# Layer 1 attention and its experts moved from two blocks of the program into one unrolled block

## What is computed

```python
xn = layernorm(x)
# attention: 16 heads of 16 features
xa = ln1(xn)
q, k, v = heads(xa @ wq), heads(xa @ wk), heads(xa @ wv)
probs = softmax(q @ k.T / sqrt(256))
s = merge(probs @ v) + xa
# experts: 2 of 8 for each token, and one shared expert
w_full = softmax over the top 2 of xn @ Wr * SCALE
h = (xn @ W1[e]) * silu(xn @ W3[e])
f = sum_e (h @ W2[e]) * w_full[e] + shared(xn)
x = x + s * silu(f)
```

## Time and profile before

| what | value |
|---|---|
| times of three runs, us | 2135.24, 2135.78, 2128.12 (median 2135.24) |
| the profiled execution, us | 2123.32, span 2121.7 |
| mean granted clock of TensorE | 0.905 of full |
| busy share of the span | PE 80%, DVE 55%, ACT 40%, POOL 25% |
| attention: first maxima to last matmul of a group | 1091.9 to 1602 us |
| experts: first transposes to the last indirect write | 1609.0 to 2063.1 us |
| finish | 2070.6 to 2121.7 us |

### The profile page before, as it was taken

The page is one execution under the profiler, slowest core; times in us unless marked ns, Lnnn a source line. Parts: engine busy times, 40 slices in busy tenths (PEclk is TensorE's granted clock), DMA queues, the critical chain, the costliest instruction groups (busy, mean ns, idle before and its releaser), DMA issues. The chain is left out here.

```text
span 2121.7 us, 24658 instructions
## 1 busy us (share of the span) xinstructions
PE 1699.5 (80%) x8146; PEld 1105.1 (52%) x8146; DVE 1175.5 (55%) x2114; ACT 850.9 (40%) x1509; POOL 529.8 (25%) x579
## 2 busy tenths in 40 slices
PE   4458999999998499999628888888776999999960
PEld 2336666666666355655302223222224888888850
DVE  3435545654565234343367677777753655666635
ACT  1124444444444121222105556666663544445421
POOL 1122524253434212212024420000000333333330
PEclk8679999999999799999858889999987999999985
DMA  4433444544433444343254542332313555555537
GB/s 132 139 110 99 100 117 114 147 105 117 96 110 60 130 152 152 140 168 119 80 129 120 147 127 78 82 86 75 89 29 100 143 148 140 144 135 128 148 60 237
DMA packets 223458, 251.08 MB, mean 118 GB/s; under 512 B 35984, under 2 KB 172688, under 8 KB 223376
## 3 DMA queue, kind: packets, MB, share of 16 engines
q1 hardware_dynamic: 193616, 208.54, 32.4%
q0 software_dynamic: 29760, 41.50, 11.1%
HBM read 153.34 MB, written 96.10 MB: 118 GB/s over the span
## 5 line engine op out<-in xcount | busy, mean ns | idle before, releaser
L1244 DVE TENSOR_REDUCE a_neg_max<-a_bank 128x1 f32<-128x512 f32 x512 | 328.4, 684 | 93.8 <-PE a_bank L1147 85.7
L1224 ACT ACTIVATE a_prob<-a_bank 128x512 f32<-128x512 f32 x512 | 278.6, 598 | 244.2 <-PE a_bank L1158 226.4
L1158 PE MATMUL a_bank<-a_qa,a_ka 50*128 50x512 f32 x512 | 135.5, 525 | 90.8 <-ACT a_prob L1224 61.0
L1476 POOL DMA_INDIRECT fs<-e_y,e_token x92 | 143.3, 1557 | 243.7 <-issue 232.5
L1147 PE MATMUL a_bank<-a_ka,a_qa 48*128 48x512 f32 x512 | 127.3, 491 | 39.6 <-DMA a_va<-v 29.3
L1577 DVE TENSOR_TENSOR e_h<-e_bank,e_sg 128x512 f32<-128x512 f32 x92 | 63.6, 692 | 167.3 <-ACT e_sg L1542 164.4
L1167 PE MATMUL a_bank<-a_prob,a_va 128*32 128x512 f32 x1024 | 155.2, 734 | 1.2 <-ACT a_prob L1224 1.2
L1158 PEld LDWEIGHTS a_bank<-a_qa,a_ka 50*128 50x128 f32 x512 | 50.7, 193 | 200.7 <-ACT a_prob L1224 111.0
L1542 ACT ACTIVATE e_sg<-e_bank 128x512 f32<-128x512 f32 x92 | 55.0, 597 | 222.3 <-PE e_bank L92 222.3
L648 POOL DMA_INDIRECT f<-e_ye,c_slot_row x64 | 101.0, 1579 | 72.7 <-issue 47.6
L895 PE MATMUL p_bank<-p_xnT,p_ws 128*128 128x512 f32 x256 | 111.2, 592 | 0.0
(11 more groups left out here) (311 smaller groups left out, 4075.4 us busy)
## 6 DMA issues: line engine op xcount, KB each, us to landing
e_raw<-in_W SPq DMA_DIRECT2D x69, 512.0 KB
e_raw<-in_w SPq DMA_DIRECT2D x48, 512.0 KB, 5.6
a_qa<-qk SPq DMA_DIRECT2D x192, 64.0 KB
a_ka<-qk SPq DMA_DIRECT2D x192, 64.0 KB
xs<-c_pad SPq DMA_DIRECT2D x23, 516.0 KB
e_xg<-xs SPq DMA_DIRECT2D x23, 516.0 KB, 3.7
qk<-p_hi SPq DMA_DIRECT2D x32, 256.0 KB, 2.0
qk<-p_lo SPq DMA_DIRECT2D x32, 256.0 KB, 2.0
```

Source lines behind the costliest of these rows:

```text
L1158: nc.tensor.matmul(SB[(c + s) % 3][:], ka[q][rows, p, j * P:(j + 1) * P], qa[q][rows, p, :], start=True, stop=True).then_inc(s_ps, 1)
L1224: nc.scalar.activation(prob[j][:, 2 * p + s, :], SB[(c + s) % 3][:], ACT.Exp, scale=float(D) ** -0.5).then_inc(p_done, 1)
L1244: nc.vector.tensor_reduce(neg_max[:, g % 2, at_:at_ + 1], MB[(c + s) % 3][:], AX.X, ALU.max, negate=True).then_inc(mx_done, 1)
L1476: nc.gpsimd.indirect_dma_start(f_rows, bass.IndirectOffsetOnAxis(token[u][:, t:t + 1], 0), y[:, t, :], None, compute_op=ALU.add).then_inc( ...
```

## The change

Both blocks become `layer1_attend_and_experts` (line 1169 of the new kernel), with all loops written out. GpSimd first scatters the rows of all 8 sequences (into `xg`, the buffer that later holds an expert group's rows). Head group g carries expert group e = g - 8 (FIRST = 8): eight *slots*, in each a score pair, a maxima pair or the turn of the maxima, and an eighth of an expert group. The down products of an expert group run one head group late. So head groups 0 to 7 carry no expert, 8 to 30 carry e = 0 to 22, and 31 carries the last down products.

With both sets of tiles in memory at once, buffers shrink: the maxima have one pair of banks (`M`, reduced as one 128x2x512 instruction; the experts' transposes use it too), the scores one pair (`S2`, one exponential of 128x1024), prob two tiles for four, qa/ka/va three for four. Silu becomes 0.5 g (1 + tanh(g / 2)), whose Tanh is on ScalarE and whose factor 0.5 went into the routing weights (line 1137), so VectorE has one more product a chunk. The low parts of the weights move from VectorE to GpSimd (line 1314), the weighting of y from VectorE to ScalarE (line 1541). The attention's result is no longer stored and loaded: GpSimd adds it to `xa_all` (`add_o`, line 1300), from two tiles `o`. `x1`, kept in on-chip memory before, is stored by `layer1_prepare` (line 829) and loaded by `finish`.

The diff, cut to its core (helpers whose body is as before are left out):

```diff
-def layer1_attention(nc, R, k, qk_v, v_v, o_v, xn_b, xs_rows):
-def layer1_experts(nc, R, k, xs_g, f_rows, w1_d, w2_d, w3_d):
+def layer1_attend_and_experts(nc, R, k, qk_v, v_v, xn_b, xs_rows, xs_g, f_rows, w1_d, w2_d, w3_d):
...
+    G, NU, NR = NB * NQ, 2 * T, 3
+    FIRST = G - 1 - NG
+    M, S2 = [R.ctx.enter_context(nc.psum_tensor(R.tag + n, [P, 2, 512], F32)) for n in ("max_bank", "score_bank")]
+    OB, YB, GATE, VALUE = R.banks(4)
...
         @block.sync
         def _(sp):
...
+            for g in range(G):
+                e = g - FIRST
+                if g + 2 < G:
+                    load_qk(g + 2)
+                if group(e + 1):
+                    load_w(0, e + 1)
+                    load_w(1, e + 1)
+                if g + 2 < G:
+                    load_v(g + 2)
+                if g + 1 < G:
+                    max_rows(g + 1)
+                if group(e + 1):
+                    load_w(2, e + 1)
+                    if e + 1 == 0:
+                        load_x(0)
+                if group(e + 2) and e + 1 >= 0:
+                    load_x(e + 2)
...
         @block.gpsimd
         def _(pool):
+            def scatter_rows(b):
+                if b:
+                    pool.wait_ge(rows_out, b * TOP * T * 16)
+                pool.dma_start(xg[:, :, 0:D], at(xn_b, b)).then_inc(rows_in, 16)
+                nc.gpsimd.tensor_copy(xg[:].bitcast(I32)[:, :, D], k.token[:, b * T:(b + 1) * T]).then_inc(marked, 1)
+                for i in range(TOP):
+                    if i:
+                        pool.wait_ge(rows_out, (TOP * b + i) * T * 16)
...
+            for b in range(NB):
+                scatter_rows(b)
+            added = 0
+            for g in range(G + 2):
+                e = g - FIRST
+                if group(e - 2):
+                    combine(e - 2, 1)
+                if group(e):
+                    low_w(2, e)
+                if e >= -1:
+                    while added < min(g, G):
+                        add_o(added)
+                        added += 1
+                if group(e - 1):
+                    combine(e - 1, 0)
+                if group(e + 1):
+                    low_w(0, e + 1)
+                    low_w(1, e + 1)
+                    marks(e + 1)
...
         @block.tensor
         def _(pe):
...
+            def weigh(g, j):
+                if j == 0:
+                    pe.wait_ge(v_in, 16 * (g + 1))
+                    pe.wait_ge(o_done, g)
...
+                scores(g, 0)
+                maxima(g + 1, 4)
+                if group(e):
+                    up_gate(e, 0)
+                    up_value(e, 0)
+                maxima(g + 1, 5)
+
+                scores(g, 1)
+                if g:
+                    weigh(g - 1, 3)
+                if group(e - 1):
+                    down(e - 1, 0)
+                maxima(g + 1, 6)
+
+                scores(g, 2)
+                if group(e):
+                    up_gate(e, 1)
+                maxima(g + 1, 7)
+                if g:
+                    transpose_o(g - 1)
+                if group(e):
+                    up_value(e, 1)
+
+                scores(g, 3)
+                if group(e - 1):
+                    down(e - 1, 1)
+                transpose_max(g + 1)
+
+                scores(g, 4)
+                weigh(g, 0)
+                if group(e):
+                    up_gate(e, 2)
+                maxima(g + 2, 0)
+                if group(e):
+                    up_value(e, 2)
+                maxima(g + 2, 1)
...
+                scores(g, 7)
+                weigh(g, 2)
+                if group(e + 1):
+                    transpose_x(e + 1)
+                if group(e - 1):
+                    down(e - 1, 3)
...
         @block.vector
         def _(dve):
...
+            def divide(g):
+                dve.wait_ge(oT_ps, g + 1)
+                v = OB[:].rearrange("p (t h d) -> p (t h) d", t=T, h=QH)
+                nc.vector.reciprocal(den[:], v[:, :, HD]).then_inc(den_done, 1)
+                dve.wait_ge(den_done, g + 1)
+                if g >= 2:
+                    dve.wait_ge(xa_done, g - 1)
+                nc.vector.tensor_tensor(o[:, g % 2].rearrange("p t (h d) -> p (t h) d", d=HD), v[:, :, 0:HD],
+                                        den[:].unsqueeze(2).broadcast_to([P, T * QH, HD]), ALU.mult).then_inc(o_done, 1)
```

More of the change, by code:

```diff
@@ new lines, in add_o, with marks @@
+            def add_o(g):
+                b, q = divmod(g, NQ)
+                pool.wait_ge(o_done, g + 1)
+                part = k.xa_all[:, b, :, q * QH * HD:(q + 1) * QH * HD]
+                nc.gpsimd.tensor_tensor(part, part, o[:, g % 2], ALU.add).then_inc(xa_done, 1)
+            def marks(e):
+                pool.wait_ge(xg_in, 16 * (e + 1))
+                if e >= 4:
+                    pool.wait_ge(f_out, 16 * GT * (e - 3))
+                    pool.wait_ge(y_done, 2 * (e - 3))
+                land(pool, k)
+                nc.gpsimd.tensor_copy(token[e % 4][:], xg[:].bitcast(U32)[:, :, D])
+                nc.gpsimd.tensor_copy(weight[e % 4][:], xg[:, :, D + 1]).then_inc(marks_set, 1)
@@ new lines, in transpose_max, with scores @@
+            def transpose_max(g):
+                if g >= G:
+                    return
+                pe.wait_ge(mx_done, NU * (g + 1))
+                nc.tensor.transpose(M[0:QH * T, 0, 0:P], neg_max[:, g % 2].rearrange("p s m -> p (s m)"), k.ident[:]).then_inc(mT_ps, 1)
+            def scores(g, u):
+                q, (j, p) = g % NR, divmod(u, 2)
+                if u == 0:
+                    pe.wait_ge(m_in, 4 * 16 * (g + 1))
+                if g or u:
+                    pe.wait_ge(p_done, NU * g + u)
+                for s in range(2):
+                    rows = slice(HALF * s, HALF * s + KR)
+                    nc.tensor.matmul(S2[:, s, :], ka[q][rows, p, j * P:(j + 1) * P], qa[q][rows, p, :], start=True, stop=True).then_inc(s_ps, 1)
@@ new lines, in _ @@
+            pe.wait_ge(k_set, 1)
+            for m in range(NU):
+                maxima(0, m)
+            transpose_max(0)
+            for m in range(4):
+                maxima(1, m)
+            for g in range(G):
+                e = g - FIRST
+                scores(g, 0)
[30 more added lines that the diff above has]
+                maxima(g + 2, 1)
+                scores(g, 5)
+                weigh(g, 1)
+                if group(e - 1):
+                    down(e - 1, 2)
+                maxima(g + 2, 2)
+                scores(g, 6)
+                if group(e):
+                    up_gate(e, 3)
+                maxima(g + 2, 3)
+                if group(e):
+                    up_value(e, 3)
+                scores(g, 7)
+                weigh(g, 2)
+                if group(e + 1):
+                    transpose_x(e + 1)
+                if group(e - 1):
+                    down(e - 1, 3)
@@ L1592, in _ @@
-            low_w(0, 0)
-            low_x(0)
-            turns(dve, turn)
-def finish(nc, R, k, fs_b, at_b, out_b):
+            for i in range(NR):
+                for s in range(2):
+                    ins = nc.vector.memset(ka[i][HALF * s + 32:HALF * s + 64].bitcast(F32), 1.0)
+            ins.then_inc(k_set, 1)
+            for m in range(NU):
+                maxima(0, m)
+            split_max(0)
+            for m in range(4):
+                maxima(1, m)
+            for g in range(G):
+                e = g - FIRST
+                maxima(g + 1, 4)
+                if group(e):
+                    hidden(e, 0)
+                maxima(g + 1, 5)
+                if group(e):
+                    low_h(e, 0)
+                maxima(g + 1, 6)
+                maxima(g + 1, 7)
+                if g:
+                    divide(g - 1)
+                if group(e):
+                    hidden(e, 1)
+                split_max(g + 1)
+                if group(e):
+                    low_h(e, 1)
+                maxima(g + 2, 0)
+                if group(e):
+                    hidden(e, 2)
+                maxima(g + 2, 1)
+                if group(e):
+                    low_h(e, 2)
+                maxima(g + 2, 2)
+                maxima(g + 2, 3)
+                if group(e):
+                    hidden(e, 3)
+                if group(e + 1):
+                    low_x(e + 1)
+                if group(e):
+                    low_h(e, 3)
```

677 lines of the change are left out of this document (287 added, 390 removed).

## The result

| | before | changed |
|---|---|---|
| median of 4 runs | 2131.68 us (2124.80 to 2135.78) | 2245.25 us (2241.68 to 2252.87) |
| ratio | | 1.0528, 95% interval 1.0495 to 1.0562 |
| profiled execution | 2123.32 us, span 2121.7 | 2245.51 us, span 2243.8 |
| mean granted clock of it | 0.905 | 0.867 |

The change makes the kernel 5.3% slower: 114 us. The forecast was 2080 us, 52 us faster, and its range ended at 2130.

What follows compares the result with a forecast made beforehand. TensorE was taken to bound the fused group at 27.0 us. Stall release at 1247, groups 4 to 7 and 23 fused groups, tail and finish gave span 2066, 56 us less, so about 2080 us; range 2035 to 2130.

Steps and rivals of the forecast that it cites:

- the one on the lock: Fused groups: GpSimd's low_w and VectorE's low_h miss each other by 0.3 to 2 us, so priced at nothing extra.
- my walk: Slot-by-slot walk of one fused group: 27.0 us of TensorE work plus waits of 0.5, 0.2 and 0.4, given as 27.9.
- the 0.9: Fused groups: 0.9 us a group added for waits that a slot-by-slot count misses.
- rival 1: Fused groups: two low_w hold a low_h each, 4.8 us a group, 110 us more, 2190 us; chance 0.06.
- 28.8 forecast: Time of a fused group, 28.8 us against 33.8 one after the other; 23 of them gain 115 us.
- the 158 us above: Account of the 23 fused groups: forecast 657 us, measured 815, difference +158.
- Half overlap: Fused groups: hand-overs cost more than walked, 30.5 to 31.7 us a group, 2119 to 2147 us; chance 0.10.
- 18.3 us: Head groups without an expert: assumed time per group, four of them costing 13 us more than at 15.0.
- The half-clock end: Head groups without an expert: 22.4 us each if TensorE runs at half clock, against 16.8 at full clock.
- the 26 us: Account from stall release to the first fused group, 4.5 groups: forecast 82 us, measured 108, difference +26.
- the stall: divide(2) waits for the first add_o behind GpSimd's row writes: about 1180 to 1247, some 65 us with TensorE idle.
- The bound of 31.7 us a group: Sign against the forecast: it is wrong if fused groups take over 31.7 us.

Runs made afterwards that it cites:

- the gate: Changed kernel with GpSimd's low_w(2, e) held back by a wait until low_h of the first chunk is done: 2136.28 us (before 2126.51).
- the kernel with adjacent products: Kernel with own results, low_w(2) wait and second maxima banks, plus value products right behind gate products in slots 2 and 6: 2051.86 us, ratio 0.9625.
- the second pair: Changed kernel with idle gate and value banks taking every second maxima pair in head groups 0 to 7: 2230.27 us (before 2129.33).
- all three mended: Changed kernel with idle tiles for first results, low_w(2) behind low_h, and second maxima banks in groups 0 to 7: 2047.44 us, ratio 0.9632.

## Why the prediction was wrong

**The step that failed** is the one on the lock: "In my walk they miss each other by 0.3 to 2 us, so I price it at nothing beyond the 0.9". A walk by durations with some 2 us of error a group can't say that two instructions of 0.7 and 2.4 us miss by 0.3. They met in 22 of 23 groups. The argument with which rival 1 got 0.06, that in a fixed phase held ones drift apart, is contradicted too: the delay holds TensorE and so moves the whole group, the next one included, and in 20 groups GpSimd's record starts 0.49 to 0.53 us behind VectorE's. Rival 1 is what happened, but that its price of 4.8 us a group, taken for two collisions, is so near the 4.74 measured is luck: it was one collision, 2.9 us of wait, and 2.2 for the clock behind it, together 5.15, and two of the 23 groups lost nothing (e = 1, held for 2.5 us, and e = 4). 4.74 x 23 = 109, as the gate gave back. The rows of before had shown the pair with GpSimd as the one held; that it also goes the other way round stood only on the page of the Trainium skill that the prediction cites. The traces show both ways: GpSimd's copies held, and VectorE held where GpSimd's subtraction starts first (2.47 us). But in the 20 groups VectorE's record starts 0.5 us ahead and VectorE is the one held, so "whichever starts first" does not describe the order of these records.

The walk's sum had a slip besides: 27.0 + 0.5 + 0.2 + 0.4 is 28.1, not 27.9, 0.2 us a group.

**TensorE's own work was too small.** In the kernel with the gate TensorE is 99% busy and still takes 30.8 us, against 28.8 forecast: the missing 2.0 are 46 us over the kernel. So of the 158 us above some 109 are the lock and 49 this. A pattern of its rows:

```profile
1815.79 0.50 PE L92 MATMUL a_bank<-a_xThi,a_w31hi 128*128 128x512 f32 x1
1816.12 0.39 PE L92 MATMUL a_bank<-a_xTlo,a_w31hi 128*128 128x512 f32 x1
1816.35 0.40 PE L92 MATMUL a_bank<-a_xThi,a_w31lo 128*128 128x512 f32 x1
...
1817.38 0.50 PE L1364 MATMUL a_max_bank<-a_ka,a_qa 48*128 48x512 f32 x2
```

Matmuls start 0.23 apart inside a run, as I had counted, but 0.33 after a change of the kind of work. The run of six from 1815.79 to 1817.38 takes 1.59, not 6 x 0.2255 = 1.35; runs of twelve down products take 1.54 to 1.62, not 1.42; a set of `weigh` 0.99, not 0.87. A fused group has 35 such runs, the old expert group three changes of kind, and a price of 0.1 each, an estimate from these starts, gives 3.5 of the 3.7 between 27.0 and 30.7; the wait of 0.23 in front of a maxima pair is the rest. In the kernel with adjacent products four runs took 0.1 less each, which fits; nothing else tests this price. My 0.9 for "waits that such a walk misses" was to cover this, and "Half overlap" (30.5 to 31.7 a group) was the right case for it.

**The groups without an expert were mis-sized.** I took 18.3 us between 16.8 and 22.4, "nearer to the full clock, as in the old attention (0.89)". Groups 4 to 7 took 23 to 25 at 0.55. Order of time, TensorE, in that stretch of the changed kernel:

```profile
1262.94 0.80 PE L1363 MATMUL a_max_bank<-a_ka,a_qa 48*128 48x512 f32 x2 [1.42 <-DVE a_neg_max L1601]
...
1264.09 1.93 PE L1388 MATMUL a_bank<-a_prob,a_va 128*32 128x512 f32 x8
...
1268.10 0.79 PE L1363 MATMUL a_max_bank<-a_ka,a_qa 48*128 48x512 f32 x2 [0.93 <-DVE a_neg_max L1601]
```

They are the earlier trace rows and not the earlier trace rows: pairs of 0.80, sets of `weigh` of 1.93, and a wait of about a microsecond at each step for the single pair of maxima. The walk had TensorE waiting at each of these steps, which the old attention with its separate banks did not the earlier trace rows, and this spoke against taking over the old attention's clock. The half-clock end, 22.4, was near; the choice cost some 16 of the 26 us (four groups by 4.1). The single pair is part of the cause, as the second pair shows; the level of the clock is as measured, and why it differs between runs of the same code is open.

**What was right:** the stall, its cause, its start and its end within 11 us; the durations of the double reduction (1.22), the double exponential (1.03) and GpSimd's subtraction (2.39); that VectorE, ScalarE and GpSimd stay off the bound; the finish within 2 us. The bound of 31.7 us a group was too high, since the front cost more than forecast: already at 30.8, without the lock, the kernel is no faster than before (2136 and 2127, one run each), at 32.4 and 35.5 it is slower.

So putting the two layers' work side by side is worth what it was for, (33.8 - 30.8) x 23 = 69 us; the stall and the slow groups around it give that back, the lock takes 109 more. With all three mended it is 2047 us.

**Still open:** why VectorE is held for the whole of GpSimd's subtraction in the 20 groups in which its own record starts 0.5 us ahead, and the indirect write in front of the subtraction still runs for 1 us, while it isn't held by the small copies in such a place; what sets the clock in the groups without an expert; how much of the 0.1 us at a seam on TensorE is loading of another kind of weights and how much the check of a semaphore.

## What to carry to other kernels

When work moves to GpSimd beside a busy VectorE, list the VectorE instructions with two SBUF inputs and the GpSimd ones that read SBUF, the pair that collided here, and don't rely on their missing each other: order them, with one semaphore if need be; here it gave back 5%. Where TensorE waits at every step, cost the stretch with rows at the half clock, and add to a wait what the clock behind it may cost. When two streams are woven on TensorE, add a price for each seam between kinds of matmuls, taken from starts and not from durations.

## What the runs showed of the hardware

- A VectorE subtraction of two SBUF tiles, 0.69 us long, took 2.47 us beside a GpSimd subtraction whose record had started 0.47 us before it, and 4.01 us beside one that started 0.49 us behind it. Both times it ended 0.55 us behind GpSimd's end, and GpSimd lost nothing. Beside a GpSimd memset, an indirect write or copies of 128x4 it kept its 0.69; the copies took 1.0 us for 0.19.
- VectorE instructions with at most one SBUF input (reductions 1.22, products 0.69) kept their durations beside the same GpSimd subtractions.
- A GpSimd record can start while the instruction before it still runs: a subtraction of 2.4 us behind an indirect write had a record of 2.96, which began 0.55 us ahead of that write's end.
- A wait of 1.4 us in TensorE once in 32.1 us left the granted clock at 1.00; one of 2.9 us in 35 to 36 was followed in the windows shown by some 5.7 us at 0.50 or 0.71.
